# A cleared column and a wait ahead of every indirect DMA of a two-layer graph kernel

## What is computed

```python
h = jnp.maximum(_layernorm(x, axis=-1), 0.0)
x = x + segment_sum((h * node_vec1)[src], dst, num_segments=12500) * node_vec1_n2
h = jnp.maximum(_layernorm(x, axis=-1), 0.0)
x = x + (1.0 + eps[0]) * h + segment_sum(relu(h[src] + edge_attr_32), dst, num_segments=12500)
```

## Time and profile before

| what | value |
|---|---|
| median of 3 runs | 4981.2 us |
| the profiled execution's own span, first to last instruction | 8580.9 us |
| its mean granted TensorE clock, as a share of full | 0.733 |
| indirect DMAs from GpSimd: scatter, gathers of layer 1, gathers of layer 0 | 1875, 1250, 480 + 50 |
| busy share of that span: TensorE, VectorE, ScalarE, GpSimd | 51%, 43%, 36%, 42% |

### The profile page before, as it was taken

How to read it: one execution, slowest core, us unless ns; L and a number is a source line. 1 busy time by engine, 2 the same in 40 slices (tenths; PEclk the granted TensorE clock), 3 DMA queues, 4 the chain that set the end, 5 groups by cost and what they waited for, 6 DMA issues and landing times.

```text
span 8580.9 us, 129759 instructions
## 1 busy us (share of the span) xinstructions
PE 4359.2 (51%) x44428; PEld 3164.9 (37%) x44428; DVE 3658.4 (43%) x11303; ACT 3124.7 (36%) x8299; POOL 3610.0 (42%) x3712
## 2 busy tenths in 40 slices
PE   0555555555555555555555555445444444545444
PEld 0333333333333333333333333334334343434343
DVE  6444444444444444444444444434343333434334
ACT  0333434343333333333333333234333333433333
POOL 7444444444444444444444444343443434343442
PEclk8777777777777777777777777666666666666666
DMA  5111111111111111111111100101110111101110
GB/s 90 31 31 31 31 31 31 31 30 31 30 31 30 31 30 31 30 31 30 31 30 31 31 17 17 43 22 31 30 32 22 32 29 32 31 22 32 30 32 17
DMA packets 437255, 265.45 MB, mean 31 GB/s; under 512 B 330740, under 2 KB 421220, under 8 KB 430120
## 3 DMA queue, kind: packets, MB, share of 16 engines
q1 hardware_dynamic: 318264, 185.91, 9.1%
q0 software_dynamic: 116960, 65.42, 4.4%
q10 hardware_dynamic: 1296, 4.79, 0.2%
HBM read 176.35 MB, written 79.52 MB: 30 GB/s over the span
## 4 chain that ended last, share of the span: by engine, by line
PE 36%; issue 26%; another core or an unknown queue 22%; DVE 9%; ACT 5%; SPq 1%; DVEq 0%; ACTq 0%; DMA 0%; POOL 0%; POOLq 0%
PE candidates L1179 16%; DVE arena L1663 5%; PE candidates L1105 5%; PE plain_ps L1191 4%; PE sorted_agg L1122 4%; DVE arena L1639 3%; PE key_rows L1074 2%; ACT centered L974 2%; PE candidates L1100 2%; ACT message L920 2%; PE plain_ps L1143 1%; PE candidates L1092 1%; ACT arena L821 1%; PE plain_ps L1151 1%
## 5 line engine op out<-in xcount | busy, mean ns | idle before, releaser
L710 POOL DMA_INDIRECT records<-stage,place_i x1875 | 1821.1, 971 | 675.8 <-issue 625.1
L698 POOL DMA_INDIRECT stage<-table,src_plain x1250 | 1193.9, 955 | 1778.1 <-DMA stage<-in_edge_attr 1386.7
L1639 DVE TENSOR_SCALAR arena<-arena,row_key 125x1280 bf16<-125x1280 f16 x1000 | 552.6, 553 | 2554.9 <-ACT arena L821 1776.0
L920 ACT ACTIVATE message<-candidates,member_is 128x96 bf16<-128x96 f32 x3600 | 912.4, 352 | 1643.5 <-remote 922.8
L691 POOL DMA_INDIRECT message<-table,mid_src x480 | 533.5, 1112 | 2234.8 <-PE plain_ps L1151 2095.5
L1105 PE MATMUL candidates<-parts,arena 125*128 125x32 bf16 x15000 | 589.2, 181 | 1214.2 <-issue 1211.8
L821 ACT ACTIVATE arena<-key_rows 125x640 f16<-125x640 f16 x1000 | 662.5, 719 | 1237.3 <-remote 987.2
L1663 DVE TENSOR_SCALAR arena<-window_iota,dst_rel 128x224 bf16<-128x224 f16 (+1 forms) x4800 | 1025.9, 280 | 112.4 <-remote 67.7
L1105 PEld LDWEIGHTS candidates<-parts,arena 125*128 125x128 bf16 x15000 | 503.7, 99 | 1384.6 <-issue 1370.1
L1092 PE MATMUL candidates<-parts,arena 125*128 125x96 bf16 x5000 | 312.0, 220 | 1312.9 <-ACT message L920 748.6
L1074 PE MATMUL key_rows<-ident,record 128*125 128x128 f16 x5000 | 494.6, 242 | 878.4 <-issue 587.7
(11 more groups left out here) (224 smaller groups left out, 5798.9 us busy)
## 6 DMA issues: line engine op xcount, KB each, us to landing
record<-records SPq DMA_DIRECT2D x50, 1650.0 KB, 7.1
stage<-in_edge_attr SPq DMA_DIRECT2D x125, 400.0 KB, 3.2
records<-pad SPq DMA_DIRECT2D x25, 1650.0 KB, 10.7
records<-stage,place_i POOLq DMA_INDIRECT x1875
stage<-table,src_plain POOLq DMA_INDIRECT x1250
message<-table,mid_src POOLq DMA_INDIRECT x480
xs<-in_x SPq DMA_DIRECT2D x8, 390.6 KB
table<-parts ACTq DMA_DIRECT2D x4, 585.9 KB
```

Of the source, the lines that this page charges most:

```text
L698: pool.indirect_dma_start(message[:, k, j, :] if l == 0 else rows[:, k, j, :], None, table0 if l == 0 else table1, bass.IndirectOffsetOnAx ...
L710: pool.indirect_dma_start(records, bass.IndirectOffsetOnAxis(ap=place_i[:, h, e:e + 1], axis=0), stage[:, h, e, :], None).then_inc(scatter ...
L920: last = nc.scalar.activation(direct_message[n % DB][:, m * WIDE:(m + 1) * WIDE], candidates[n % 2][:, m * WIDE:(m + 1) * WIDE], ACT.Copy, ...
L1639: nc.vector.tensor_scalar(src_onehot[:, g % 2, o, :], key_row[:, g % 2, :], row_key[0:NP, o:o + 1], None, ALU.is_equal).then_inc(src_oneho ...
```

## The change

A scratch tile `pause_room` of one column and a semaphore `pool_paused` are added (an unused one goes). A helper clears the column on GpSimd, waits on GpSimd until that is done, and adds one to a semaphore that nobody waits for. It is called ahead of each of the 75 scatters and 20 gathers of a batch in layer 0 and of the 50 gathers of a batch in layer 1. The 50 gathers of layer 0's last batch and the loops for far edges, which don't run here, keep their form.

```diff
+        pause_room = sb("pause_room", [P, 1])
...
+            PAUSES = SE + MID
+
+            def pause(nth):
+
+                pool.memset(pause_room[:], 0.0).then_inc(pool_paused, 1)
+                pool.wait_ge(pool_paused, nth + 1)
+                pool.sem_inc(gathers_begun, 1)
+
-            def gather_mid(h):
+            def gather_mid(b, h):
                 pool.sem_inc(gathers_begun, 1)
                 for j in range(MID):
+                    pause(PAUSES * b + SE + j)
                     pool.indirect_dma_start(
...
-            def gather(l, k, tiles, landed, indices):
+            def gather(l, k, tiles, landed, indices, pauses=None):
                 pool.sem_inc(gathers_begun, 1)
                 for j in tiles:
+                    if pauses is not None:
+                        pause(pauses + j)
                     pool.indirect_dma_start(
...
                     if is_first(b) and e % J == 0:
                         pool.wait_ge(first_ranked, e // J + 1)
+                    pause(PAUSES * b + e)
                     pool.indirect_dma_start(
...
-                    gather(1, k, range(J), gathered[1][k], src_plain[:, k, 0:J])
+                    gather(1, k, range(J), gathered[1][k], src_plain[:, k, 0:J], PAUSED0 + PJ * b + k * J)
```

More of the change, by code:

```diff
@@ L368, in gnn_two_layers @@
         nodes_ready = sem("nodes_ready")
-        xs_steps = sem("xs_steps")
+        pool_paused = sem("pool_paused")
         result_ready = sem("result_ready")
@@ L693, in gather_mid @@
                         bass.IndirectOffsetOnAxis(ap=mid_src[:, h, j:j + 1], axis=0)).then_inc(gathered[0][0], 16)
-            def gather(l, k, tiles, landed, indices):
+            PAUSED0 = PAUSES * (BATCHES - 1) + SE
+            def gather(l, k, tiles, landed, indices, pauses=None):
                 pool.sem_inc(gathers_begun, 1)
                 for j in tiles:
+                    if pauses is not None:
+                        pause(pauses + j)
                     pool.indirect_dma_start(
@@ L730, in step0 @@
                         pool.wait_ge(plain_done[0], b)
-                    gather_mid(h)
+                    gather_mid(b, h)
             over_batches(pool, step0)
```

## The result

The changed kernel takes 7384.2 us, the median of four runs from 7381.6 to 7386.4; the kernel before took 4979.9 beside it. The ratio is 1.482, with a 95% interval of 1.480 to 1.484. 7430 us were predicted. The time grew by 2404 us, or 0.667 us for each of the 3605 pauses; 0.68 had been predicted.

The account below looks back on a forecast made before the run. GpSimd's chain of DMAs was taken as the bound in both layers; 3605 pauses at 0.68 us give 2451 us, which on 4981 makes 7432 us (7430 likeliest). The range was 6050 to 8400 us.

Parts of the forecast that it names:

- The sum of GpSimd's DMAs: GpSimd in both layers: 3655 DMAs one after the other, 4700 us, plus 210 us of idle, 4910 us together.
- The sum of the others: Other engines: 150 us to the first record, 25 x 119, 25 x 47 and some 180 at seams, 4480 us.
- the seams: Term of the other engines' total: some 180 us at seams, beside their batches in both layers.
- DMA's end to the clear: Start of a pause on GpSimd: 0.07 us between the DMA ahead ending and the queued clear, bounds 0.03 to 0.30.
- the clear's end to the DMA: End of a pause on GpSimd: 0.81 us from the wait's release to the DMA, read from gathers released by middle products.
- gap that it takes the place of: Between neighbouring DMAs on GpSimd before the change: 0.30 us idle, which the pause replaces.
- The profiled execution: Profile after the change: span grows from 8581 by 2451 to about 11030 us, less what other engines do in pauses.
- A: Rival, chance 0.09: the DMA is made ready during the wait, so a pause costs 0.27 us; 5954 us.
- B: Rival, chance 0.08: GpSimd isn't the bound in a median run, having 1260 us of slack; its chain grows to 6170 us.
- C: Rival, chance 0.04: each clear waits out a large VectorE instruction at shared ports; a pause costs up to 1.23 us, 9400 us.
- D: Rival, chance 0.04: slower DMAs free TensorE from its stall beside the scatters, so time falls, down to 4480 us.
- E: Rival, chance 0.02: nothing to measure, as the compiler merges or drops the wait or slack swallows it; 4981 us.

Follow-up runs that it names:

- e5: The kernel before, unchanged, run for a second profile of it: 4983.5 us, with a profiled span of 4981.7 us.
- e7: The kernel before, no pauses, with 50 of the 75 scatters and 13 of the 25 gathers of a unit in layer 1: 4519.9 us, ratio 0.907.
- e8: The changed kernel with clear, wait and increment done twice ahead of each DMA: 8353.5 us, ratio 1.677 to the kernel before.
- e4: The changed kernel with layer 0's pauses taken out, leaving 1250 pauses in layer 1: 5806.8 us, ratio 1.165 to the kernel before.
- e6: The kernel before, no pauses, with 70 of the 75 scatters and 23 of the 25 gathers of a unit in layer 1: 4700.5 us, ratio 0.944.
- e3: The changed kernel, but each wait is for the clear of the pause before, with three columns taking turns: 5084.4 us, ratio 1.020 to the kernel before.
- e1: The changed kernel without the clear; GpSimd's sequencer adds to the semaphore itself and waits for that: 4980.7 us, ratio 0.999 to the kernel before.

## Why the prediction was right

**The bound.** It rested on sums made against the median, from an execution that didn't look like a median run. The sum of GpSimd's DMAs, 4910 us, was right to 1.4%, for a reason that is half luck: gaps and busy times together came to 3655 DMAs at 1.28 us and 210 us beside them, where e5 has means of 1.35 (scatters), 1.31 and 1.28 (gathers), some 150 us more, and 132 us beside them (30 at the start, 52 at the seam, 50 after the last gather), some 80 less. The sum of the others, 4480 us against 4520 in e7, is half luck too. Of its terms, 119 us for a batch of layer 0 was 118.3 in e7, but 47 for one of layer 1 was 53.5, from these stretches of two batches and of the last four:

```profile
2359.90:2596.50 236.60, 217.78 (x1839) 149.64 (x1838) 195.77 (x593) 163.74 (x478) 143.60 (x140) 0.99 0.26 53
4217.00:4431.00 214.00, 180.00 (x3394) 159.20 (x3390) 180.51 (x591) 169.25 (x390) 98.94 (x101) 0.90 0.19 57
```

Over the whole layers, from one batch's first matmul that turns keys (L1074) to the next one's, e7 has 118 and 56.5 us. So layer 1 was put some 240 us too short: busy times at full clock leave out that no engine is busy all the time (TensorE and VectorE, the busiest, are so for 84% of the second stretch, at a clock of 0.90). What then is left for the seams is some 16 us, not 180, and that made up for most of it. GpSimd's lead was also spread otherwise: 127 against 118 us a batch and 65.5 against 56.5, 9 in either layer, where the prediction's figures, 120 against 119 and 63 against 47, give 1 and 16. It decided nothing, since GpSimd is the longer in both.

**The pause, term by term.** Measured over all 3605 pauses after, and in e5 for the gap before:

| term | predicted, us | measured, us |
|---|---|---|
| DMA's end to the clear | 0.07 | 0.01 |
| the clear | 0.10 | 0.14 |
| the clear's end to the DMA | 0.81 | 0.83 |
| the DMA's own length, after against before | 0.96 to 0.96 | 1.02 to 1.02 |
| gap that it takes the place of | 0.30 | 0.30 |
| sum, a pause | 0.68 | 0.67 |

The single row that carried the sum was the gather released by the middle products, 0.81 us. Of the two ends for the first term the one of a clear behind a clear, 0.03, was the nearer. Both periods were taken too short, by 0.07 and 0.05 us (means of 1.33 and 1.99): the single DMAs that I read, 0.96 us, stood beside an idle VectorE, and the mean DMA lasts 1.02. In the difference this all but fell out.

**Who waits.** A batch takes 191 us in layer 0 and 99 in layer 1 (184 and 97 predicted), and the others fit into that, with TensorE's clock at a mean of 0.78 over the span.

**The profiled execution** was predicted at 11030 us and came at 7384.6. The step that failed is that I let the first profile's stall stand as something that the next profile would show again. Its durations served, its idle times were of that one execution.

**The rivals.** A (0.27 us, 5954) is what a wait costs in front of a plain instruction: e8's second pause has just that price. B (GpSimd not the bound, the 0.30 us due to the profiled execution) falls with e5, where the same gap stands in an execution as long as a run, and with e4 and e6. C (the lock) asked for up to 0.55 us on a clear: the mean clear is 137 ns, against a median of 113. D (faster) needed TensorE's stall in a median run: e5 doesn't have it (TensorE is busy for 79% of its span, 51% in the earlier trace rows). E falls with the result.

## What to carry to other kernels

Before a wait or an instruction is put into an engine's row, ask what that engine was making ready behind its back: here 0.68 us of each DMA's preparation lay beside the DMA ahead, and any wait for work that ends after it brings them out, while a wait for older work cost 4% of that (e3, nearly all of it in 54 gaps) and one met at once nothing (e1). If a profiled execution is much longer than the runs, take its durations and orders, add them up for each engine, and see which sum meets the measured time; a second profile is cheap. To size a wait, look for the same kind of instruction behind a wait elsewhere in the trace, not for the wait itself.

## What the runs showed beyond that

The stretched execution of the kernel before, 8580.9 us against 4981.7 for the same program, showed TensorE at 111 matmuls in 95 us beside the scatters; the changed kernel, the second profile of before and all other kernels showed nothing of the kind. What stretched it stays open.

After the change a gap of some 3 us stands in GpSimd's row once a batch in layer 0 and about once in two batches in layer 1; in layer 0 it is always ahead of the 19th of the 20 gathers (us in total, times, longest; the second row holds shorter ones too):

```profile
POOL message L701 <- issue: 71.6, 23, 3.1
POOL stage L712 <- issue: 64.9, 35, 3.2
```

In e5 the longest such gap was 0.3 us. The register instructions place it: 30 times the next one starts 2.9 to 3.0 us after the wait and not 0.57, in the change as in e8 and e3, and no such gap stands in e1, which has the same register instructions. Its cause wasn't tried; against the 0.8 us of an ordinary pause it makes 23 x 2.3 = 53 us of the 2404 in layer 0.
